# Language-model tower: VectorE's subtractions over eight slots, causal statistics in slots 0 and 1, an early table load on ScalarE

## What is computed

```
sr = (qr kr' + qi ki') * scale ;  si = (qi kr' - qr ki') * scale
scores = sqrt(sr * sr + si * si)
probs  = softmax(scores, axis=-1)          # 12 heads of 16 features
h      = h + probs v
x      = layernorm(layernorm(h))           # input of the causal attention
```

## Time and profile before

| | us |
|---|---|
| median of 3 runs | 1079.2 (1076.35 to 1081.35) |
| profiled execution | 1093.29 |
| its span, first to last instruction | 1091.6 |
| TensorE busy | 955.4 (88%) |
| ScalarE busy | 676.2 (62%) |
| VectorE busy | 669.9 (61%) |
| mean granted TensorE clock | 0.91 of full |

### The profile page before, as it was taken

How to read it: one execution, slowest core, us unless ns; L and a number is a source line. 1 busy time by engine, 2 the same in 40 slices (tenths; PEclk the granted TensorE clock), 3 DMA queues, 4 the chain that set the end, 5 groups by cost and what they waited for, 6 DMA issues and landing times.

```text
span 1091.6 us, 22081 instructions
## 1 busy us (share of the span) xinstructions
PE 955.4 (88%) x7209; PEld 732.6 (67%) x7210; DVE 669.9 (61%) x3063; ACT 676.2 (62%) x1438; POOL 460.3 (42%) x508
## 2 busy tenths in 40 slices
PE   2487878988998899999999999766999999999996
PEld 2355555655656566676677766555888888888896
DVE  2577778987988766776777675583343343443432
ACT  2148768968989878787788887463344344444431
POOL 7776646650110011312312122304666667667654
PEclk7668889989999989998999998757999999999999
DMA  7433323231002000011011102235554346454342
GB/s 207 80 57 60 54 50 63 50 50 30 14 19 59 2 2 2 2 35 35 6 31 35 35 16 50 68 52 80 75 102 87 80 101 85 79 106 84 48 51 29
DMA packets 63364, 59.24 MB, mean 54 GB/s; under 512 B 17406, under 2 KB 54304, under 8 KB 63264
## 3 DMA queue, kind: packets, MB, share of 16 engines
q0 software_dynamic: 25344, 27.89, 18.1%
q1 hardware_dynamic: 37728, 29.85, 10.4%
q10 hardware_dynamic: 192, 0.26, 0.1%
HBM read 35.28 MB, written 16.39 MB: 47 GB/s over the span
## 4 chain that ended last, share of the span: by engine, by line
PE 69%; DVE 10%; ACT 6%; SPq 5%; issue 4%; POOL 2%; DMA 2%; another core or an unknown queue 1%; POOLq 0%; DVEq 0%; ACTq 0%
PE ps_scores L768 13%; PE ps_ring L760 13%; PE ps_ring L1015 9%; PE ps_ring L768 8%; PE ps_scores L886 6%; PE ps_ctx L903 5%; PE ps_scores L889 4%; PE ps_scores L1015 4%; SPq L493 4%; PE ps_ring L840 1%; PE ps_ring L839 1%; ACT square L1113 1%; DVE probs L1397 1%; DMA k<-k_signed 1%; ACT probs L1122 1%
## 5 line engine op out<-in xcount | busy, mean ns | idle before, releaser
L1234 ACT ACTIVATE probs<-ps_scores,fc_bias 128x512 f32<-128x512 f32 (+1 forms) x144 | 88.0, 616 | 148.8 <-PE ps_scores L768 143.9
L642 POOL DMA_INDIRECT out<-z_t,slots_now x80 | 135.4, 1693 | 103.6 <-DVE z_t L1708 74.0
L1104 ACT ACTIVATE prob_t<-ps_ring 128x512 f32<-128x512 f32 x192 | 114.2, 597 | 43.6 <-PE ps_ring L760 40.3
L760 PE MATMUL ps_ring<-ident,probs 128*128 128x128 f32 x768 | 128.1, 293 | 5.1 <-ACT k L1084 1.9
L1129 ACT ACTIVATE probs<-probs,neg_max 128x128 f32<-128x128 f32 x384 | 121.5, 396 | 7.6 <-DVE neg_max L1397 7.6
L1113 ACT ACTIVATE square<-ps_scores 128x512 f32<-128x512 f32 x192 | 104.8, 601 | 28.7 <-PE ps_scores L886 23.1
L1397 DVE CUSTOM_DVE_ANT_0 probs<-ps_scores,causal 128x128 f32<-128x128 f32 x384 | 88.6, 286 | 52.8 <-PE ps_scores L889 52.6
L1015 PE MATMUL ps_ring<-work,probs 128*128 128x192 f32 x672 | 115.9, 328 | 5.7 <-ACT probs L1234 5.4
L1015 PEld LDWEIGHTS ps_ring<-work,probs 128*128 128x128 f32 x672 | 109.2, 190 | 9.4 <-issue 9.4
L1391 DVE CUSTOM_DVE_ANT_0 probs<-square 128x128 f32<-128x128 f32 x384 | 89.4, 287 | 39.9 <-ACT square L1113 38.2
L768 PE MATMUL ps_scores<-x_hi,fc_hi 128*128 128x512 f32 (+1 forms) x288 | 105.8, 373 | 7.3 <-DVE x_hi L1692 3.6
(11 more groups left out here) (215 smaller groups left out, 2218.9 us busy)
## 6 DMA issues: line engine op xcount, KB each, us to landing
k<-k_signed SPq DMA_DIRECT2D x176, 32.0 KB
work<-pj_w SPq DMA_DIRECT2D x8, 576.0 KB
token_in<-xin SPq DMA_DIRECT2D x8, 384.0 KB, 3.2
out<-resid SPq DMA_DIRECT2D x8, 384.0 KB, 4.0
vals<-fc_w SPq DMA_DIRECT2D x8, 384.0 KB
vals<-fc_w SPq DMA_DIRECT2D x16, 192.0 KB
out<-z_t,slots_now POOLq DMA_INDIRECT x80
token_in<-xin SPq DMA_DIRECT2D x8, 128.0 KB, 4.1
```

The source lines that it names most:

```text
L642: gp.indirect_dma_start(out[:, :], bass.IndirectOffsetOnAxis(slots_now[:, u, 1, t:t + 1], 0), slot_y[:, o, :], None, compute_op=ALU.add).t ...
L760: return pe.transpose(dst, src, ident[0:n, 0:n])
L1104: sc.activation(prob_t[:, s % 2, :, :], src.rearrange("p (h q) -> p h q", h=4), ACT.Exp if p is mag else ACT.Copy).then_inc(ring_free[i], 1)
L1234: sc.activation(hidden[:, c % 2, f_, 0:128 * nt], ps_scores[:, i, 0:128 * nt], ACT.Gelu, bias=fc_bias[:, e, f_:f_ + 1]).then_inc(gelu_done ...
```

## The change

Three edits. VectorE's subtractions: two jobs in each of the slots 13, 14 and 15 of the pass itself instead of three, and one in each of the slots 0 to 5 of the next pass instead of one in each of the slots 2 to 4. The causal statistics stand in slots 0 and 1 and their gathering in slot 2, instead of 2, 3 and 4. ScalarE gets an exponential of one element a partition, of a column of a constant tile, behind the last root of a group and ahead of the fills of slot 15.

```diff
+        one_exp = sb("one_exp", [128, 1])
...
                     if now is not None and now < GROUPS and slot >= 12:
                         roots(now, slot - 12)
+                        if slot == 15:
+                            sc.activation(one_exp[:, :], ln_c[:, 0:1], ACT.Exp)
...
                 stats_done, in_done = cau.named("moments_stats"), cau.named("x_in")
-                if slot in (2, 3):
-                    if slot == 2:
+                if slot in (0, 1):
+                    if slot == 0:
 
                         dve.wait_ge(mag.ctx_done, GROUP * (g + 1))
-                    for s in (2 * (slot - 2), 2 * (slot - 2) + 1):
+                    for s in (2 * slot, 2 * slot + 1):
                         last = ve.bn_stats(stats[:, s, :], resid[:, GROUP * g + s, :])
                     last.then_inc(stats_done, 1)
-                elif slot == 4:
+                elif slot == 2:
...
                     if now is not None and now < GROUPS and slot >= 13:
-                        for j in range(3 * (slot - 13), 3 * (slot - 13) + 3):
+                        for j in range(2 * (slot - 13), 2 * (slot - 13) + 2):
                             shift_rows(now, j)
-                    if ready is not None and ready < GROUPS and 2 <= slot < 5:
-                        shift_rows(ready, slot + 7)
+                    if ready is not None and ready < GROUPS and slot < 6:
+                        shift_rows(ready, slot + 6)
```

## The result

| | before | after |
|---|---|---|
| median, 20 executions each | 1082.87 us (1076.35 to 1088.97) | 1078.41 us (1071.61 to 1083.34) |
| ratio, 95% interval | | 0.9948 (0.993 to 0.9967) |
| profiled execution | 1093.29 us, span 1091.6, clock 0.91 | 1077.97 us, span 1076.3, clock 0.92 |

By the ratio the change takes 0.52% off, about 5.6 us of 1082.9; the two medians differ by 4.5 us. On another chip the ratio was 0.994 (0.9909 to 0.9971). That is at the edge of what can be told from no change; both intervals exclude 1. I had forecast 2.1 us, so the direction held and the range too, and the size was short by a factor of two to three.

A forecast was written before the change was run, and what follows sets the result against it. No engine is full everywhere; waits at group turns of the first attention bound it, with keys limiting gains. 1.0 + 0.7 + 0.4 + 0.2 - 0.2 = 2.1 us off 1079.2 gives 1077.1; range 1070.5 to 1082.5.

The forecast's parts named there:

- The gate of the keys: Scores of job 2 wait for turned keys: nothing kept at three group turns, those waits growing to about 1.0 us.
- 5 to 6: Turn from group 5 to group 6 of the first attention: kept 0, still 18.5 us from key copy to scores.
- 2 to 3: Turn from group 2 to 3: three subtractions fewer ahead of `xn`, on which TensorE waits 1.65 us; kept 1.0 us.
- The sign named for it: In the profile after, TensorE's wait for `xn` at the turn from group 2 to 3 should be gone.
- The maxima of job 0: VectorE's row maxima behind a turn: 308.3 against 307.87 us, costed at nothing, with about 2 us of cover.
- 4 to 5: Turn from group 4 to 5: 0.8 to 1.6 us of room before scores of job 2; kept 0.7 us.
- 7 to 8 and the causal passes: Statistics moved earlier: 0.4 us at the turn from group 7 to 8, 0.2 us in all in the causal passes.
- The dummies: Added one-element exponentials cost 0.1 us each at the turns 0 to 1 and 1 to 2: -0.2 us.
- The drain rule: Rival: about 1.38 us of drain per table switch, the load holding ScalarE longer; 8 us slower, 1087; chance 0.02.
- a rival of 7.9 us: Shorter waits keep TensorE's clock up at two turns: gain 2.1 + 4.3 + 1.5 = 7.9 us, 1071.3; chance 0.24.
- a change of over 0.01: Sign of being wrong: the granted clock moves by over 0.01 in the profile after.

The follow-up runs named there:

- e4: Changed kernel with the eight key transfers of block 2 issued by GpSimd instead of SyncE from group 4 on; ratio to before 0.995.
- e8: Changed kernel with the query copy on VectorE and block 2's key transfers issued by GpSimd from group 4 on; ratio to before 0.9936.
- e6: Changed kernel with the causal statistics back in slots 2 and 3, so subtractions and load only; ratio to before 0.9971.
- e7: Changed kernel with the query copy of slot 15 on VectorE instead of ScalarE in all eight magnitude groups; ratio to before 0.9952.
- e5: The changed kernel as it is, run again on the second chip; ratio to before 0.994.
- e1: Kernel before with only the causal statistics moved to slots 0 to 2; ratio to before 1.0014.
- e3: Kernel before with only the one-element exponential added, so the table load stands behind the last root; ratio to before 0.998.
- e12: Changed kernel with two more table loads (one-element root and exponential) behind the one it has, at each magnitude turn; ratio to before 1.018.

## Why the prediction was right, and where it fell short

*The gate of the keys: right.* That 5 to 6 would still take 18.5 us from key copy to scores, that the waits for keys would grow to about 1.0, and that these turns would keep nothing: 18.64, and 1.17, 1.21 and 0.77. The 0.13 between 18.64 and 18.51 says nothing, as the same distance is 18.14 to 18.78 in the other kernels in which these scores wait for keys. From the first key copy of group 6 to that of group 7, which has this turn in it, it is 37.7 us before (291.75 to 329.45) and 37.8 after (280.29 to 318.12), both at full clock. e4 and e8 show that it is the keys: with the relief the pass is 1.3 us shorter.

*2 to 3, 1.0 us: right in size.* The pass with that turn took 37.7 us before (173.13 to 210.85 by the key copies) and 36.8 after (166.28 to 203.11), both at full clock: 0.9. The third transpose of probabilities came 1.2 earlier behind the key copy (13.79 against 15.01), as worked out. Three other kernels with the subtractions and the load moved pass here at full clock, e6, e7 and e8, with 37.1, 36.8 and 37.3, so the gain is 0.4 to 0.9. The sign named for it, the wait for `xn` gone, did not come: 0.74 of it is left.

*The maxima of job 0: right.* I put them at 0.4 later and at no cost. At 5 to 6 they are 16.52 behind the key copy against 16.12, and no square of ScalarE waits for maxima in the turns from 2 to 3 on.

*4 to 5, 0.7 us: too much, by the reading of the room.* I took the scores at 272.89 and found 0.8 to 1.6 us of room before the keys would land. But the clock had fallen at 268 there, so TensorE was late for a reason of its own. The kernel with the statistics alone shows the same turn of the old kind at full clock, with the key copy at 248.40 and scores of job 2 at 266.56:

```profile
257.05 0.50 PE L768 MATMUL ps_ring<-x_hi,w_hi 128*128 128x512 f32 x1 [1.26 <-DVE ctx_n L1336]
261.07 0.66 PE L760 MATMUL ps_ring<-ident,xn 128*128 128x128 f32 x4 [1.25 <-ACT prob_t L1104]
262.46 0.66 PE L760 MATMUL ps_ring<-ident,probs 128*128 128x128 f32 x4 [0.38 <-DVE x_hi L1288]
```

and e5, the changed kernel, with the key copy at 249.27:

```profile
260.71 0.66 PE L761 MATMUL ps_ring<-ident,probs 128*128 128x128 f32 x4 [1.09 <-ACT q L1073]
262.59 0.66 PE L761 MATMUL ps_ring<-ident,probs 128*128 128x128 f32 x4 [0.38 <-DVE x_hi L1291]
266.95 0.71 PE L887 MATMUL ps_scores<-k,q 32*128 32x256 f32 x8 [0.19 <-DMA k<-k_signed]
```

By the transposes ahead of job 1 the change has won 0.74 (14.06 against 13.32 behind the key copy), as forecast. At the scores of job 2 it is 0.48, as they wait 0.19 for the keys now (18.16 against 17.68). At the next group's key copy it is 0.14 (36.76 against 36.62). What took the last 0.34 I haven't found; it is spread over gaps that are each small.

*7 to 8 and the causal passes, 0.6 us together: not shown, and the wait at 7 to 8 misleads.* The wait for maxima at 7 to 8 fell from 1.32 to 0.23:

```profile
375.78 0.91 PE L890 MATMUL ps_scores<-k,q 32*128 32x128 f32 x8 [0.23 <-DVE neg_max L1400]
```

The statistics are not what shortened it. With them alone (e1) it is 1.30, and with the load alone (e3) 0.21. What differs is the clock: it came back to 2.4 GHz 3.0 us ahead of these scores in before and 3.2 in e1, but only 0.7 ahead in the changed kernel and 0.4 in e3, so there TensorE came late and had less to wait for. What the statistics do give is seen on VectorE: from the start of the second low halves to the first maxima it takes 1.91 us in the changed kernel and e1 and 2.14 in before and e6, so 0.2, where I had said 0.3 to 0.4. In the other causal passes the waits fell to 0.59, more than I had counted on. But e1 shows no gain at all. I had read one wait and not asked what the pieces moved ahead would delay, the low halves.

*The dummies, -0.2:* not to be told apart from zero. Their row is 0.11 before the next instruction starts, as taken.

*The drain rule, given 0.02:* the exponential loads take 1.28 us and the next instruction starts 0.02 later, even with three loads in a row (e12). Of what the Trainium skill ("ScalarE: Activation LUTs", What ACT_TABLE_LOAD costs) states, the length of the load agrees and the drain does not show.

*The clock: the term that was mis-sized.* The sum had the clock at nothing and kept it apart as a rival of 7.9 us. It is neither. In many executions the clock rose by 0.004, which goes with 2.9 of the 4.5 us by which the mean span fell on the second chip. The rest, 1.5 us and uncertain by 0.5, is what the turns gave, against my 2.1. So the turns' own sum is not refuted; the size came out too small because the clock stood in it at nothing. I named a change of over 0.01 as the sign that I was wrong. At 0.7 us for each 0.001 that is 7 us, more than the whole effect, so the sign was set far too coarse. It was also set on one profile, and the two profiles do move by 0.010, from 0.910 to 0.920, more than half of which is the spread of single executions.

*Luck.* The forecast time, 1077.1, is only 1.3 us from the measured 1078.41. It started from 1079.2, the median of three runs, 3.7 below the median of 20, and that more than made up for the 2.4 by which the gain was short.

## What to carry to other kernels

When an edit shortens an engine's stalls, price the stall and the clock that it brings down: add eight stalls on purpose and read time and mean clock over many executions, as one profile can't show it. Before counting room behind a transfer, or reading a wait as shorter or gone, see whether the engine was at full clock there. And where a chain of small DMAs on one queue ends a stage at a low DMA share, split the issuing between queues along with shortening the rest: here the mean span fell by 0.5 us with the split alone (not to be told from nothing), 4.5 with the change, 5.7 with both, and 7.4 with the query copy as well, though not all on one chip.

## What the runs showed of the hardware

- The time of one program follows the mean granted clock from execution to execution: 0.69 to 0.77 us for each 0.001, over clocks of 0.908 to 0.930. The line takes in about 80% of the variance of the span between executions of one kernel, whose range is 12 to 16 us for the kernel before. The profile of before that I worked from had 0.910 and a time 10 us above the median of its 20 executions.
- A table load costs 1.28 us wherever it stands, and three of them with one-element operations between took 1.50, 1.51 and 1.40 us from start to the start of what followed.
- Taking all table loads out of the magnitude groups, 2.6 us of ScalarE in each, brought 3.3 us in all, and 0.5 of it at equal clock.
